# Transposes moved into the banks of the turned scores, and the turned scores moved behind the first unit of a round

## What is computed

```python
xn = _layernorm(x)
# attention and experts
qkv = (xn @ W_qkv + b_qkv).reshape(B, S, 3, H, hd)
attn = softmax(einsum("bqhd,bkhd->bhqk", q, k) / sqrt(hd))
attn_out = einsum("bhqk,bkhd->bqhd", attn, v).reshape(B, S, D)
combine = sum(one_hot(top_i, E) * top_g[..., None], axis=2)
moe_out = einsum("bsef,bse->bsf", einsum("bsd,edf->bsef", xn, W_experts) + b_experts, combine)
# state-space branch
u = conv(xn @ W_in + b_in)
h = tanh(A) @ h + u_t * Bp ;  y_t = Cp @ h + Dp * u_t
out = x + silu(y) @ W_out + b_out + attn_out + moe_out
```

## Time and profile before

| what | us |
|---|---|
| runs of the kernel | 814.09, 810.25, 803.99 |
| their median | 810.25 |
| the profiled execution, its own time | 812.04 |
| its span in the trace, first to last instruction | 810.2 |
| mean granted clock of TensorE in it | 0.978 of full speed |
| PE busy / DVE busy / ACT busy / POOL busy | 744.3 / 578.9 / 530.4 / 396.5 |

### The profile page before, as it was taken

The page is one execution under the profiler, slowest core; times in us unless marked ns, Lnnn a source line. Parts: engine busy times, 40 slices in busy tenths (PEclk is TensorE's granted clock), DMA queues, the critical chain, the costliest instruction groups (busy, mean ns, idle before and its releaser), DMA issues.

```text
span 810.2 us, 17055 instructions
## 1 busy us (share of the span) xinstructions
PE 744.3 (92%) x6318; PEld 526.2 (65%) x6318; DVE 578.9 (71%) x845; ACT 530.4 (65%) x926; POOL 396.5 (49%) x522
## 2 busy tenths in 40 slices
PE   9887899989998899988999889999989889999997
PEld 7665677756775666666776566766666556766664
DVE  6656787867868675696866768587877779667840
ACT  5523677766766757657666665767757657677785
POOL 8433475544643634444635444444535336445664
PEclk9968999999999999999999999999999999999999
DMA  8301011112111121111311012111312012112100
GB/s 273 56 6 42 27 41 42 42 41 75 29 32 40 41 73 40 33 31 40 93 41 42 16 51 67 43 40 40 94 27 54 23 31 56 42 41 70 38 2 27
DMA packets 32480, 39.34 MB, mean 49 GB/s; under 512 B 8513, under 2 KB 18535, under 8 KB 32398
## 3 DMA queue, kind: packets, MB, share of 16 engines
q1 hardware_dynamic: 31418, 37.29, 17.7%
q10 hardware_dynamic: 980, 0.96, 0.5%
HBM read 8.74 MB, written 4.19 MB: 16 GB/s over the span
## 4 chain that ended last, share of the span: by engine, by line
PE 60%; DVE 20%; issue 10%; ACT 5%; POOL 3%; DMA 1%; SPq 0%; ACTq 0%; DVEq 0%; POOLq 0%
PE PS L622 21%; PE PS L599 11%; PE PS L746 10%; DVE mx L1180 7%; PE SB L702 7%; PE TB L722 5%; DVE ys L1035 3%; PE PS L646 2%; DVE ys L1031 2%; DVE qkl L1061 2%; DVE xn L1157 2%; POOL acc L1248 1%; ACT mt L809 1%; PE PS L753 1%; DVE xTl L1048 1%
## 5 line engine op out<-in xcount | busy, mean ns | idle before, releaser
L1180 DVE TENSOR_REDUCE mx<-SB 128x2 f32<-128x1024 f32 x256 | 312.9, 1222 | 136.1 <-PE SB L702 135.0
L1248 POOL TENSOR_TENSOR acc<-acc,mt 128x256 f32<-128x256 f32 x320 | 255.7, 807 | 173.7 <-ACT mt L809 121.7
L962 ACT ACTIVATE Pt<-TB 128x1024 f32<-128x1024 f32 x250 | 257.9, 1031 | 116.5 <-PE TB L722 114.8
L702 PE MATMUL SB<-kst,qst 48*128 48x512 f32 x512 | 132.8, 438 | 10.3 <-DVE mx L1180 9.0
L809 ACT ACTIVATE mt<-PS,cpad 128x256 f32<-128x256 f32 x256 | 106.8, 476 | 31.2 <-PE PS L599 30.0
L722 PE MATMUL TB<-qst,kst 50*128 50x512 f32 x500 | 121.8, 402 | 1.7 <-ACT Pt L962 1.6
L746 PE MATMUL PS<-Pt,V 128*17 128x512 f32 x1024 | 123.3, 599 | 0.0
L622 PE MATMUL PS<-weh,xTh 64*128 64x512 f32 x254 | 104.5, 412 | 13.3 <-DVE at L1091 3.7
L599 PE MATMUL PS<-weh,xTh 64*128 64x512 f32 x254 | 106.8, 421 | 0.0
L622 PE MATMUL PS<-wel,xTh 64*128 64x512 f32 x254 | 101.1, 398 | 0.0
L599 PE MATMUL PS<-wel,xTh 64*128 64x512 f32 x254 | 101.0, 398 | 0.0
(11 more groups left out here) (215 smaller groups left out, 1987.6 us busy)
## 6 DMA issues: line engine op xcount, KB each, us to landing
qst<-qkh SPq DMA_DIRECT2D x124, 64.0 KB, 2.3
kst<-qkh SPq DMA_DIRECT2D x124, 64.0 KB, 2.3
out<-acc SPq DMA_DIRECT2D x8, 512.0 KB, 2.8
qst<-qkl SPq DMA_DIRECT2D x62, 64.0 KB, 2.2
kst<-qkl SPq DMA_DIRECT2D x62, 64.0 KB, 2.3
acc<-in_x SPq DMA_DIRECT2D x7, 512.0 KB, 4.5
Bt<-in_wexp SPq DMA_DIRECT2D x2, 512.0 KB, 9.1
raw<-in_wexp SPq DMA_DIRECT2D x2, 512.0 KB, 8.3
```

The source lines that it names most:

```text
L702: ins = e.matmul(SB[:, h, :], qst[rows, g % 3, jj, 128 * a:128 * a + 128], kst[rows, g % 3, jj, :], start=True, stop=True)
L962: e.activation(Pt[:, T % NP, :, :], turned_bank(T)[:, :, :], ACT.Exp, scale=0.25).then_inc(s_ex, 1)
L1180: e.tensor_reduce(mx[:, g % 2, 0:2, 4 * jj + a], SB[:, :, :], AX.X, ALU.max).then_inc(s_mx, 1)
L1248: e.tensor_tensor(v, v, mt[:, item % NM, :], ALU.add).then_inc(s_mt, 1)
```

## The change

1. X, P, T and C in rounds 2 to 255 no longer take one of the three banks. P and the second T go to the upper bank of `TB` (number 4), the others to the lower one (number 3). Such a unit waits for the exponential of its own round's turned scores (`s_ex`), and the next `turned` waits until the units in `TB` have been read (`TURNED_AFTER`).
2. In a round with one split unit, `turned` now stands behind that unit and no longer ahead of it. With two or more units nothing changes: `turned` stays behind the first. In a round without split units it still stands right behind `score`.
3. P stands ahead of X.
4. What ends in a value round is read late in that same round by every engine, not early in the next one; before, the last unit of the round (P, the second T, C) was read in the next round, behind the next `largest` on DVE.
5. DVE does its early units ahead of the taps of `conv`.
6. `SETTLE` goes from 1500 to 1100.
7. Both matmuls of a `score` or a `turned` count up their semaphore, and the waits are doubled accordingly.

The values stand where they stood. Core of the diff:

```diff
-SETTLE = 1500
+SETTLE = 1100
...
+        g = normal_at(t)
+        if g is not None:
+            row.append(("P", g // 4, g))
...
-    finish = {u: (t, t + (k == len(row) - 1)) for t, row in ends.items() for k, u in enumerate(row)}
+    finish = {u: (t, t + (u == row[-1] and not values_at(t))) for t, row in ends.items() for u in row}
...
-            bank = min((j for j in range(3) if j != open_), key=lambda j: used[j])
-            used[bank] = place[key]
+            if kind in "XPTC" and 1 < t < STEPS:
+                bank = 4 if kind == "P" or key[::2] == ("T", 1) else 3
+            else:
+                bank = min((j for j in range(3) if j != open_), key=lambda j: used[j])
+                used[bank] = place[key]
...
+TURNED_AFTER = {}
+for _u in UNIT.values():
+    if _u.bank > 2:
+        TURNED_AFTER.setdefault(max(_u.t + 1 - LAG, 0), []).append(_u)
...
-    return ENDS[t - 1][-1:] if t - 1 in ENDS else []
+    return ENDS[t - 1][-1:] if t - 1 in ENDS and not values_at(t - 1) else []
...
-    return ENDS[t][:-1] if t in ENDS else []
+    return ENDS[t] if values_at(t) else ENDS[t][:-1] if t in ENDS else []
...
-        OB, FB = PS[0], PS[1:4]
+        OB = PS[0]
...
+        FB = [P[:, :] for P in PS[1:4]] + [TB[:, h, :] for h in range(2)]
...
+                if u.bank > 2 and u.t >= LAG:
+                    e.wait_ge(s_ex, u.t - LAG + 1)
...
+                for u in TURNED_AFTER.get(t, ()):
+                    e.wait_ge(*bank_read(u))
...
-                between = [u for u in AT[t] if u.split][1:]
-                if LAG <= t < STEPS + LAG and not between:
+                first = next((u for u in AT[t] if u.split), None)
+                if LAG <= t < STEPS + LAG and first is None:
                     turned(t - LAG)
...
-                    if between and u is between[0] and LAG <= t < STEPS + LAG:
-                        turned(t - LAG)
                     if u.split:
                         bank_there(u)
                         operands_there(u)
                         side_by_side(u)
+                        if u is first and LAG <= t < STEPS + LAG:
+                            turned(t - LAG)
...
+                for u in early(t):
+                    if u.kind != "D":
+                        unit(u)
                 for s in (3, 2, 1, 0):
                     for b, d in y_read(t - s - 1):
                         conv(b, d, s)
-                for u in early(t):
-                    if u.kind != "D":
-                        unit(u)
```

More of the change, by code:

```diff
@@ L131, in plan @@
             load(*u, t)
+        g = normal_at(t)
+        if g is not None:
+            row.append(("P", g // 4, g))
+            load(*row[-1], t)
+            spent -= COST["P"]
         g, rest = divmod(t - 8, 8)
@@ L136, in plan @@
             spent -= COST["X"]
[L137 to L141, removed]
         bare = fixed(t) < 1.5 and not any(COST[u[0]] > 0.5 for u in row)
@@ L192, in plan @@
             open_ = None
-    finish = {u: (t, t + (k == len(row) - 1)) for t, row in ends.items() for k, u in enumerate(row)}
+    finish = {u: (t, t + (u == row[-1] and not values_at(t))) for t, row in ends.items() for u in row}
     place = {u: n for n, u in enumerate(u for row in ends.values() for u in row)}
-    units, item, uses, frees, held = {}, 0, [0] * 3, [0] * 3, [None] * 3
+    units, item, uses, frees, held = {}, 0, [0] * 5, [0] * 5, [None] * 5
     used, open_ = [-9] * 3, None
@@ L387, in program @@
         s_S, s_ST, s_PV = sem("S_done"), sem("ST_done"), sem("PV_done")
-        s_full, s_low = [sem(f"bank_full{i}") for i in range(3)], sem("lower_rows_done")
+        s_full, s_low = [sem(f"bank_full{i}") for i in range(5)], sem("lower_rows_done")
         s_kx, s_kr = sem("krylov_mm"), sem("response_mm")
-        s_free = [sem(f"bank_free{i}") for i in range(3)]
+        s_free = [sem(f"bank_free{i}") for i in range(5)]
         s_hi = [sem(f"w_hi{i}") for i in range(9)]
@@ L470, in half_stack @@
             if g >= 3:
-                e.wait_ge(s_ST, 8 * (g - 2))
+                e.wait_ge(s_ST, 16 * (g - 2))
             else:
@@ L633, in bank_there @@
                     e.wait_ge(*bank_read(u.before))
+                elif u.bank > 2:
+                    e.wait_ge(s_kp, 1)
+                    e.wait_ge(s_kv, 17)
+                if u.bank > 2 and u.t >= LAG:
+                    e.wait_ge(s_ex, u.t - LAG + 1)
             def unit(u):
@@ L701, in score @@
                         rest_of_ahead()
-                    ins = e.matmul(SB[:, h, :], qst[rows, g % 3, jj, 128 * a:128 * a + 128], kst[rows, g % 3, jj, :],
-                                   start=True, stop=True)
-                ins.then_inc(s_S, 1)
+                    e.matmul(SB[:, h, :], qst[rows, g % 3, jj, 128 * a:128 * a + 128], kst[rows, g % 3, jj, :],
+                             start=True, stop=True).then_inc(s_S, 1)
                 pair_behind()
@@ L721, in turned @@
                         rest_of_ahead()
-                    ins = e.matmul(turned_bank(t)[:, h, :], kst[rows, g % 3, jj, 128 * a:128 * a + 128], qst[rows, g % 3, jj, :],
-                                   start=True, stop=True)
-                ins.then_inc(s_ST, 1)
+                    e.matmul(turned_bank(t)[:, h, :], kst[rows, g % 3, jj, 128 * a:128 * a + 128], qst[rows, g % 3, jj, :],
+                             start=True, stop=True).then_inc(s_ST, 1)
                 pair_behind()
@@ L956, in _ @@
                 if 0 <= T < STEPS:
-                    e.wait_ge(s_ST, T + 1)
+                    e.wait_ge(s_ST, 2 * T + 2)
                     if T >= NP:
@@ L1176, in largest @@
                 g, a, jj = t // 8, t % 8 // 2, t % 2
-                e.wait_ge(s_S, t + 1)
+                e.wait_ge(s_S, 2 * t + 2)
                 if t % 8 == 0 and g >= 2:
```

## The result

The changed kernel takes 829.04 us, median of 4 runs (827.91 to 829.42); the kernel before, run beside it, has 807.59 (803.99 to 814.09). The ratio is 1.0264, with a 95% interval of 1.0218 to 1.0309: slower by 21.4 us, where 12.8 were forecast. Of all executions here one, of `f2_mixed_apart`, ran in a slow state (1151.09 us at a granted clock of 0.556), and it stands in no comparison. The profiled execution took 829.31 us, its span is 827.5.

What follows compares the result with a forecast made beforehand. PE's work plus its waits for readers of its banks was taken as the bound; 812.0 + 36.5 + 5 + 3 + 4 - 28 - 5 - 1.7 - 1 = 824.8 us, or 823.0 on the median's scale; range 803 to 843.

Steps and rivals of the forecast that it cites:

- Adjacency: Value rounds behind one-unit rounds: turned pair waits for ACT's exponential, 37 times 1.05 us less 2.4, +36.5 us.
- rival (b): Stall behind a lone unit is cushioned as next waits shrink: 0.7 us each, bank gains of 35, 801 us; chance 0.22.
- nothing gained or lost: Other one-unit rounds: turned pairs stay 1.85 us apart, exponential with its lead takes 1.5, so no change in time.
- Banks: X, P, T, C leave the three banks: PE's waits for readers of Q, P and T go, -28 us.
- DVE's order: DVE reads early units ahead of the convolution's tap, so PE waits less for V's and Q's readers: -5 us.
- P and T read ahead of the maximum: DVE reads P, T before the next maximum: later maximum in 26 rounds, +5 us; wait for `xTl` in 7, +3 us.
- P's wait for its exponential: Value rounds with P: exponential late by 0.5 us in a quarter of 31 rounds, +4 us.
- clock: One mid-span half-clock stretch behind P's wait of 2.1 us goes: half of 3.3 us, -1.7 us.
- `SETTLE`: With doubled semaphore counts and counting order, moves single products of narrow V and O units by one place: -1 us.
- rival (d): Clock falls: each of 37 new stalls brings 3.3 us at half clock, 61 us in all, 884 us; chance 0.03.
- (a): Bank waits come back as waits for the maximum; half of the 33 us is lost, 840 us; chance 0.22.
- (c): Faster: exponential parted from the `mt` copies, 131 rounds gain 0.2 us, value rounds don't wait for it, 789 us; chance 0.09.

Runs made afterwards that it cites:

- f2_mixed_apart: Changed kernel, turned pair placed by surrounding rounds; in 8 stretches behind each lone unit, then between the next value round's two sets of values: 802.1 us, ratio 0.9907.
- first experiment: Kernel before with only the turned pair moved behind the first unit, no other part of the change: 853.17 us, ratio 1.0566.

## Why the prediction was right, and where it was small

The direction, the mechanism and the place were right: the turned pair behind a lone unit leaves only a score between it and the next, PE waits for the exponential (29.5 us, where 30 to 40 were forecast), and the banks give back less than that. Slower by over 2% had a chance of 0.40 in the prediction; the change is 2.6% slower.

- **Adjacency, +36.5 us forecast.** Alone it costs 44.5 us by the medians and 39.5 between the two traces (first experiment); this is the term that was too small. Its place and cause were right, and the sum behind it was right in part by luck. The stall was sized well where nothing else changes: 1.04 us in the 12 value rounds without units, against 1.05 forecast. But it isn't 1.05 in all 37. In rounds 16 to 249 there are 35 such value rounds, and they are 29.9 us longer in all: 1.10 each in the 4 with C, 0.90 in the 4 with T, and 0.63 in the 15 with X and P, where P's wait for Q's reader fell from 4.4 to 1.5 us. So some of the stall is cushioned, as rival (b) has it. The 2.4 us that I took off for scores that wait for the maximum aren't there: that wait is 2.4 us in these rounds before and 2.3 after. On the other side I held the other one-unit rounds at "nothing gained or lost". The 71 of them that stand behind no value round are 0.11 us longer, 8.0 us in all, and the 54 rounds with two or three units take 3.0 us more. The `mt` copies now come behind the later exponential, but PE's wait for them grew mostly in the rounds with two or three units and is only 0.8 us in the 71. The 8.0 us weren't traced to a wait, and their cause stays open.
- **Banks, -28 us; DVE's order, -5; P and T read ahead of the maximum, +5 and +3; P's wait for its exponential, +4; clock, -1.7; `SETTLE`, -1.** Together -23.7; measured together 853.17 - 829.04 = 24.1 less. The sum is right, and the parts less so. The -28 us were put down to the banks alone; the runs give 13.6 to the banks once the rest is there and some 10.5 to the rest, in which P's place and the reading in the same round are worth 8 to 9 in the kernel before. DVE's order was 4.1. P ahead of the maximum cost 0.03 us in each of 28 rounds and not 0.2: `mh` runs beside `at`, which I had in series. For T, +3, the 6 one-unit rounds behind it take 2.76 us in the changed kernel and 2.77 with the turned pair moved alone: nothing. P's wait for the exponential hardly exists: P starts 0.58 us behind the end of its round's exponential on the mean, and at 0.10, the least, in 2 of 29 rounds. `SETTLE` was 0.4, which the runs don't tell from nothing.
- **Clock.** I counted two stretches at half clock behind the first 90 us of the kernel before; its trace has a third, at 286.5 us, behind a wait of 1.6 us. All three run at full clock now, and one is new, at 594.0 us, behind a wait of 1.78 us for the maximum. So one is left, as forecast, though not one of the old. Two more of before, at 64.6 and 78.3 us, are gone too. That is four stretches of 3.4 us fewer from trace to trace, some 7 us by my estimate and not 1.7. Part of that is no effect of the change, since the granted clock of the kernel before goes from 0.975 to 0.986 from one execution to the next. That the drops follow waits of about 2 us, as rival (d) says, is loose: the kernel before waited 1.86 us at 358.9 us and 1.71 at 590.0, and no drop followed. Two of the old stretches, now:

```profile
246.00:255.50 9.50, 8.80 (x72) 6.14 (x72) 9.50 (x14) 6.86 (x12) 5.32 (x6) 1.00 0.17 41
255.80:259.10 3.30, 3.30 (x29) 1.64 (x22) 3.01 (x6) 1.35 (x3) 0.58 (x1) 1.00 0.00 0
...
453.80:457.10 3.30, 2.47 (x20) 1.60 (x20) 3.30 (x4) 2.14 (x4) 2.86 (x4) 1.00 0.02 5
```

- **Rivals.** (d), the clock falling behind 37 short stalls, didn't happen: the mean granted clock went from 0.978 to 0.987. By what the Trainium skill reports of frequent short idles ("TensorE: Matmul & The Clock Gate", section "A second HAM failure mode: psum-queue depth-cycling") it would have. This trace doesn't agree: 33 waits of 0.9 us on the mean did not do it here. (a), waits for the maximum in place of bank waits, is there in small: 12.1 against 9.0 us. The first experiment refutes (b) as it was priced, though P's wait for Q's reader did shrink, and it refutes (c), a gain in the one-unit rounds.

## What to carry to other kernels

When a producer's buffer is single, count the work between two of its uses at every seam of the schedule: moving the producer behind some work in most rounds puts two uses side by side wherever the pattern changes, and the price is the consumer's whole latency less what is left between them. A round that is wide enough to hold the producer in its middle is the place to change over. Look for the cheap part of a bundle: here the order of two small transposes and reading them in the same round was worth 8 to 9 us alone, and was hidden under a part that cost 44.

## What the runs showed that was not expected

The transposes in `TB` bring 13.6 us with the turned pair behind the unit. With it ahead of the unit, where the next turned pair comes right at their readers, they seem to cost time; how much is not shown, since the 9 us measured there hold other parts too. A stall costs more than its idle row: the pair behind it lasts 0.50 us instead of 0.40. And a wait's row is not the time that its removal brings. Halving one operation on ACT moved PE's wait row and the kernel's time by the same 13.6 us. With the values set apart the same row fell by 29.1 us and the time by 5.3 only, since the next user of the same exponential then waited for it.
